# The Newton iteration of a landmark attention with its head pairs in one group instead of two

## What is computed

```python
kernel1 = softmax(Q @ K_l^T)      # 256 x 64 for each head
kernel2 = softmax(Q_l @ K_l^T)    # 64 x 64
kernel3 = softmax(Q_l @ K^T)      # 64 x 256
V = kernel2^T / max(column sums)
for _ in range(6):
    KV = kernel2 @ V
    V = (0.25 * V) @ (13*I - KV @ (15*I - KV @ (7*I - KV)))
SV = (kernel1 @ V) @ (kernel3 @ values)
x = x + SV @ w_proj
```

## Time and profile before

| quantity | value |
|---|---|
| median of three runs | 2761.87 us |
| profiled execution, its own time | 2772.52 us |
| its span in the trace | 2770.8 us |
| mean granted TensorE clock | 0.937 of full |
| busy: PE, PEld, DVE, ACT, POOL | 2229.7, 1674.0, 1893.1, 914.3, 797.3 us |
| landmark attention, first to last L1560 | 1185.4 to 2481.0 us |

### The profile page before, as it was taken

The page is one execution under the profiler, slowest core; times in us unless marked ns, Lnnn a source line. Parts: engine busy times, 40 slices in busy tenths (PEclk is TensorE's granted clock), DMA queues, the critical chain, the costliest instruction groups (busy, mean ns, idle before and its releaser), DMA issues.

```text
span 2770.8 us, 68027 instructions
## 1 busy us (share of the span) xinstructions
PE 2229.7 (80%) x28681; PEld 1674.0 (60%) x28681; DVE 1893.1 (68%) x4262; ACT 914.3 (33%) x2460; POOL 797.3 (29%) x831
## 2 busy tenths in 40 slices
PE   2998889889898777688888888888888888886775
PEld 2885555555687455466666666666666666664553
DVE  4666887887666899655666565665565665658996
ACT  1441000000244545333333333343343333334543
POOL 1004666766100222122222232222232222221221
PEclk9999999999999899789999999998999999987998
DMA  3000000000000000000000000000000000000002
GB/s 87 1 1 1 1 1 1 1 1 1 1 1 1 1 1 1 1 2 2 2 2 2 2 3 2 2 2 2 2 2 2 2 2 2 2 2 1 1 1 61
DMA packets 14559, 14.55 MB, mean 5 GB/s; under 512 B 1392, under 2 KB 12080, under 8 KB 14256
## 3 DMA queue, kind: packets, MB, share of 16 engines
q1 hardware_dynamic: 14256, 10.20, 1.3%
HBM read 6.01 MB, written 4.19 MB: 4 GB/s over the span
## 4 chain that ended last, share of the span: by engine, by line
PE 48%; DVE 29%; ACT 8%; issue 7%; POOL 6%; SPq 0%; DVEq 0%; POOLq 0%; DMA 0%
PE acc L683 6%; PE acc L466 5%; PE acc L1560 5%; PE acc L443 4%; PE acc L1549 4%; POOL arena L871 4%; DVE arena L835 3%; DVE arena L828 3%; ACT arena L1308 2%; PE acc L699 2%; DVE arena L838 2%; PE acc L1523 2%; ACT arena L884 2%; ACT arena L1327 2%; DVE arena L1159 2%
## 5 line engine op out<-in xcount | busy, mean ns | idle before, releaser
L1409 POOL TENSOR_TENSOR arena<-arena 128x288 f32<-128x288 f32 (+1 forms) x384 | 264.2, 705 | 878.0 <-ACT arena L1327 876.5
L630 POOL TENSOR_TENSOR arena<-arena,headcol 128x1024 f32<-128x1024 f32 x128 | 238.3, 1892 | 374.9 <-DVE arena L535 374.9
L683 PE MATMUL acc<-arena 128*128 128x512 f32 x512 | 269.4, 610 | 46.6 <-DVE arena L560 45.5
L1149 DVE SCALAR_TENSOR_TENSOR arena<-arena,acc 128x288 f32<-128x288 f32 (+1 forms) x384 | 154.4, 409 | 205.4 <-ACT arena L1327 196.2
L871 POOL TENSOR_TENSOR arena<-arena 128x960 f32<-128x960 f32 (+2 forms) x70 | 118.0, 1685 | 591.1 <-DVE arena L838 585.5
L1560 PE MATMUL acc<-arena 64*64 64x72 f32 x6144 | 244.4, 227 | 53.1 <-DVE arena L1149 51.9
L1560 PEld LDWEIGHTS acc<-arena 64*64 64x64 f32 x6144 | 218.5, 141 | 91.3 <-ACT arena L1327 71.3
L1549 PE MATMUL acc<-arena 64*64 64x72 f32 x6144 | 236.8, 228 | 9.5 <-DVE arena L1159 8.6
L1549 PEld LDWEIGHTS acc<-arena 64*64 64x64 f32 x6144 | 208.8, 135 | 48.3 <-issue 15.5
L1327 ACT ACTIVATE arena<-acc 128x288 f32<-128x288 f32 x384 | 150.4, 411 | 209.1 <-PE acc L1549 197.4
L1159 DVE SCALAR_TENSOR_TENSOR arena<-acc,arena 128x288 f32<-128x288 f32 (+1 forms) x384 | 151.5, 408 | 74.2 <-PE acc L1560 62.6
(11 more groups left out here) (230 smaller groups left out, 4495.3 us busy)
## 6 DMA issues: line engine op xcount, KB each, us to landing
out_dram<-X SPq DMA_DIRECT2D x4, 1024.0 KB, 9.3
wi<-in_wiT_dram SPq DMA_DIRECT2D x1, 256.0 KB, 2.7
wout<-in_woT_dram SPq DMA_DIRECT2D x1, 256.0 KB, 3.3
wqkv<-in_w_qkv_dram SPq DMA_DIRECT2D x1, 192.0 KB, 2.7
arena<-in_w_down_dram SPq DMA_DIRECT2D x1, 176.0 KB, 2.4
arena<-in_w_gate_dram SPq DMA_DIRECT2D x1, 128.0 KB, 2.2
arena<-in_w_up_dram SPq DMA_DIRECT2D x1, 128.0 KB, 2.7
wq<-in_WqT_dram SPq DMA_DIRECT2D x1, 64.0 KB, 2.2
```

Of the source, the lines that this page charges most:

```text
L630: pool.tensor_tensor(qx[s][:, q * NQ:(q + 1) * NQ, :], qkT[s][:, 0, :].unsqueeze(1).broadcast_to([P, NQ, SEQ]), headcol[:, q * NQ:(q + 1) ...
L683: pe.matmul(bank[s][1 + u % 2], qkT[s][:, 1, j * P:(j + 1) * P], qx[s][:, q * NQ:(q + 1) * NQ, j * P:(j + 1) * P], start=True, stop=True)\
L1409: pool.tensor_tensor(tm[s][:, group[g], cols], pm[s][:, group[g], cols], sq[s][:, group[g], cols], ALU.subtract).then_inc(tm_ready, 1)
```

## The change

GR, the number of groups into which the eight head pairs of the iteration are split, is 1 instead of 2. All the loops `for g in G` then run once, over all eight pairs, and the semaphores count one increment where they counted two.

```diff
@@ -1047,7 +1047,7 @@
             halves = [(slice(0, LM), slice(0, LM)), (slice(LM, P), slice(LM, P))]
             NMAX3, SUM3, R3, MAX2, SUM2, R2, COL, RD = range(8)
-            GR = 2
+            GR = 1
             G = range(GR)
             PG = NP // GR
             group = [slice(g * PG, (g + 1) * PG) for g in G]
```

## The result

| quantity | before | after |
|---|---|---|
| median | 2761.55 us (2760.11 to 2764.32, 4 runs) | 2907.94 us (2886.80 to 2910.56, 4 runs) |
| ratio of the runs | 1 | 1.0508 (95%: 1.0463 to 1.0552) |
| profiled execution's own time | 2772.52 us | 2886.80 us (one of the 4 runs) |
| granted TensorE clock, landmark attention | 0.93 | 0.90 |

What follows compares the result with a forecast made beforehand. It took the landmark attention as a relay between engines, PE holding 48% of the chain. Waits 79 plus clock 30 gave 109 us over the profiled 2772.52, so 2881; less 10.65, 2870 us, range 2832 to 2892.

Steps and rivals of the forecast that it cites:

- The waits: PE's later starts through the landmark attention's steps: 2.3 us a round, 69 over 30 rounds, plus 10 for first and last sequence.
- The split into steps 0 to 2 and 3 to 5: Share of the round's lateness by iteration step: 1.00 us late after step 2, 2.3 us late by factors.
- the durations at 576 elements: Merged instructions in the iteration: 0.65 us on ACT and 0.76 us on DVE.
- the unchanged cover at `even`: Between turn2 and multiply 3, PE's other work hides even as one 512-element instruction at 0.69 us; uncovered it would cost 0.7.
- POOL's cover: POOL's tm, at most 1.59 us, hides behind remainder and cube before newton; uncovered it would cost at most 0.8 a step.
- the clock's term: A second half-clock stretch over cube 4 or multiply 5 in most rounds: 0.94 us a round, 30 us; bounds 0 and 1.9 a round.
- from the profiled execution to the median: Last step of the sum: the median taken as 10.65 us below the profiled execution, turning 2881 into 2870.
- Only the waits: Rival: later starts on PE but no second low stretch, 2841 us; chance 27%.
- Faster: Rival: larger instructions cost less, saving 0.5 us a round at the fifth step, 15 us, 2747 us; chance 5%.
- the straight line through the earlier trace: Estimate of 576-element times from smaller instructions: 0.84 ns an element on ACT, 1.06 on DVE.
- no change: Rival: work of neighbouring sequences on PE hides all the added delay, 2762 us; chance 3%.
- More than I think: Rival: both matmul groups at low clock, or instructions at twice their row (1.3 us a round), about 2905 us; chance 7%.

Runs made afterwards that it cites:

- e7: Changed kernel (one group) with project repeated three times more, turn3 of quad 2 four times more, last cube over all 72 columns: 2803.1 us, ratio 1.0140.
- e6: Kernel before (two groups) with project repeated twice more, turn3 of quad 2 four times more, last cube over all 72 columns: 2714.4 us, ratio 0.9817.
- e9: The changed kernel run once more with nothing altered: median 2904.5 us, its profiled execution 2916.5 us.
- e1: Kernel before with project repeated twice more before cube 4 and turn3 of quad 2 three times more before factors: 2773.9 us, ratio 1.0037.
- e3: Changed kernel with only the wait before cube 4 filled, by project repeated three times more: 2905.3 us, ratio 1.0514.

## Why the prediction was wrong

**The waits were right.** Their sum was 79 us; e7 less e6 is 88.7. By rounds 2.42 instead of 2.3 (72.6 instead of 69), the first sequence 5.8 instead of 3 (first `scores1` at 1222.6 against 1216.8) and the last 9.0 instead of 7 (35.8 against 26.8 us between the last two `scores1`); 1.5 more come behind the last `scores1`. The split into steps 0 to 2 and 3 to 5 came out as worked out, and so did the durations at 576 elements, the unchanged cover at `even`, and POOL's cover. Before `multiply` 5 e7 has 0.21 us of the forecast 0.3; in the changed kernel itself the work between `cube` 4 and `multiply` 5 runs at half clock and takes the place of the wait. The list of PE's waits left out the one of 0.25 us before `columns` (L1496), which the later `cube` 4 takes up.

**The step that failed is the clock's term, 30 us.** Measured by e6 and e7, the clock costs the kernel before 2761.6 - 2714.4 = 47 us and the changed kernel 2907.9 - 2803.1 = 105: the change added 58 us. With the two kernels as they ran beside e6 and e7 (2765.1, and e9's 2904.5) it added 51. (The wider cube of e6 and e7 hides some 3 us in both, which the difference doesn't feel.) The prediction took one matmul group at half clock in each round, 0.94 us, with 1.9 a round as its upper bound. For the new short stretch that was right: its place is over `cube` 4 and `multiply` 5, behind a wait of 2.36 us, which take 1.49 and 1.98 us instead of 1.22 each, 1.03 together. Rounds say the same: with their short stretches they took 43.97 us, 2.3 above the undisturbed 41.64, and in the kernel before 40.49, 1.3 above 39.21. (In about every second round of before the stretch lasts 6.8 us, and the round takes 41.5.)

What the term put at nothing, without a reason, are the long low stretches, of which the change makes more. The two profiled executions of the changed kernel have 4 and 11 of them. That of the kernel before has two, one around its first `scores1` and this one:

```profile
1914.80:1928.20 13.40, 12.36 (x132) 8.92 (x130) 5.37 (x12) 2.21 (x6) 1.58 (x2) 0.50 0.01 2
```

The round into which it runs took 45.17 us instead of 40.49. So a long stretch costs 4.7 us in either kernel, for `scores1`, `back`, `multiply` 0 and `cube` 0 all run at half clock in it. I took all low stretches as short ones and priced the new one by a single row, although that very row stands in a long stretch. What makes one long is open: PE worked for 12.4 of those 13.4 us, much of it with thin matmuls (on 32 rows, or 8 columns wide) and short waits between them, but that these are the reason wasn't tried. In the changed kernel and e9 all 13 stretches that begin 40.1 us after `scores1` run on, and those that begin at 39.0 to 40.0 end after 3.4 us.

**The same mistake shows at a second place: from the profiled execution to the median.** I subtracted 10.65 us because the kernel before's runs lie that much below its profiled one. The profiled execution of the changed kernel took 2886.8, 114 us more than that of before, where 109 was forecast. That this looks right is luck: of these 114 us 89 are waits and 25 the clock, and the two executions drawn lie at opposite ends, for the one of before has the lowest mean granted clock on record of that kernel (0.937 where the others have 0.938 to 0.944), and the one of after the highest of its own (0.922). The other timed runs of after lie 10 to 24 us above it, and in e9 10 to 31 us below the one profiled there. The distance is no property of the measurement: it is 2 us at most in e6 and e7, where the clock hardly falls in this layer. The times of the timed runs follow their mean granted clock, as e9 shows; how many long stretches each had isn't recorded. The 32 us by which this step was off are not to be added to the clock's 21 to 28: they are mostly the same long stretches, seen from the profiled executions.

**The rivals.** "Only the waits" (2841) would have needed the clock to stay; with almost no low stretch, the waits alone give 2803 against 2714. "Faster" is out by the straight line through the earlier trace rows, which held, and "no change" by the new waits. "More than I think" (2905, 7%) had the size, but by another way: instructions weren't longer, and `cube` 4 and `multiply` 5 lost 1.03 us together, where that rival has both in full, 1.9.

The Trainium skill ("TensorE: Matmul & The Clock Gate", section "HAM oscillation — how this bites in real kernels") has the direction: idle time between bursts, then a burst at half clock. This trace agrees, with a new low stretch behind a wait of 2.36 us, although the section speaks of longer idle times than any wait here. Following it gave the better of the two sums.

## What to carry to other kernels

A split into two groups pays where the work that lies between two dependent steps on the bounding engine is shorter than the whole chain of the others: compare, place by place, the cover in the trace with the chain at full size; here that gave 2.3 of 2.42 us a round. Then ask what the new waits do to the TensorE clock, and price it from whole rounds with a short and with a long low stretch, not from one instruction: here a short one cost 1.3 us, and a long one 4.7 more; the trace of before already had a round with a long one. When timed runs of one kernel spread by 1%, or the profiled execution is off the median, compare the mean granted clock of the executions. Repeating harmless matmuls in the waits, if it fills enough of them, removes the low stretches, tells the waits' own price, and here made the kernel faster; filled in part (e1, e3) it gained nothing.

## What was not expected of the hardware

- Matmuls that compute nothing new made a kernel 1.8% faster (e6): the granted clock from 1300 to 2350 us was 1.00 where it had been 0.93.
- The last cube costs 1.10 us with 8 columns and 1.22 with 72. In e1 it was thin, and low stretches began shortly behind it; in e6, with it wide and one repeat more, none did. Which of these two it was wasn't tried apart.
- The same program has executions of 2885 and 2917 us, at a mean granted clock of 0.922 and 0.908; its two profiled ones have 4 and 11 long low stretches.
